# A perceiver block on one core: state-space output projection in plain float32, the gate's low part on GpSimd alone, running products behind the multiplication by the gate

## What is computed

```
proj = h @ in_proj_w.T                        # h: 128 x 512
gate, hBC, dt = split(proj)                   # gate: 128 x 8192
hBC = silu(causal_conv(hBC, 4 taps) + b)      # hs 128 x 8192, B and C 128 x 1024 each
dt = softplus(dt + dt_bias);  X = hs * dt     # 128 heads of 64 columns
M  = (C B^T) * exp(segsum(-exp(A_log) * dt))  # per head, lower triangle: 128 x 128
y  = M @ X + D * hs
xg = y * silu(gate)
xr = xg * rsqrt(mean(xg^2 over a group) + eps)   # 8 groups of 1024 columns
x  = x + (xr * norm_weight) @ out_proj_w.T       # 8192 x 512
```

## Time and profile before

| what | value |
|---|---|
| time, median of 3 runs | 752.7 us |
| the 3 runs | 751.5, 752.7, 756.2 us |
| the profiled execution | 755.4 us |
| its span, first to last instruction | 753.3 us |
| busy share of the span: PE, DVE, ACT, POOL | 95%, 74%, 52%, 40% |
| mean granted clock of PE | 0.982 of full speed |
| read from memory | 93.17 MB, 124 GB/s over the span |

### The profile page before, as it was taken

One profiled execution on the slowest core, in us unless ns is written; L12 is line 12 of the kernel. 1 busy time (PEld: TensorE's weight loads), 2 busy tenths in 40 slices (PEclk: granted clock), 3 DMA queues, 4 the chain that ended last, 5 costly groups with the idle time before them and its releaser, 6 DMA issues.

```text
span 753.3 us, 11908 instructions
## 1 busy us (share of the span) xinstructions
PE 712.1 (95%) x3929; PEld 599.1 (80%) x3929; DVE 553.7 (74%) x1159; ACT 393.6 (52%) x602; POOL 304.9 (40%) x166
## 2 busy tenths in 40 slices
PE   5899999999999999999999999779789999999996
PEld 4678888888888888888888888659778888888885
DVE  6877668658748748747857766468979887888894
ACT  4364445535536546446446444635666666665662
POOL 3352313404404504503413321100577877877772
PEclk9999999999999999999999999898989999999999
DMA  9502021011011001102201104803868777878520
GB/s 330 221 24 70 1 70 65 4 70 56 14 55 70 14 14 63 63 0 70 70 0 70 56 0 194 283 1 118 288 242 333 278 287 277 307 269 298 211 110 14
DMA packets 20290, 93.73 MB, mean 124 GB/s; under 512 B 2608, under 2 KB 3760, under 8 KB 11440
## 3 DMA queue, kind: packets, MB, share of 16 engines
q1 hardware_dynamic: 20272, 93.50, 34.4%
HBM read 93.17 MB, written 0.33 MB: 124 GB/s over the span
## 4 chain that ended last, share of the span: by engine, by line
PE 69%; DVE 16%; issue 6%; ACT 5%; DMA 2%; DVEq 1%; ACTq 0%; SPq 0%; POOL 0%; POOLq 0%
PE bank L379 17%; PE bank L381 17%; PE bank L380 17%; PE bank L489 8%; DVE conv L1282 5%; PE bank L576 3%; DVE decay L1234 2%; ACT y_gT_hi L922 2%; PE bank L459 2%; DMA ctx_raw<-in_ctx_t 1%; DVE y_gT_lo L1269 1%; DVE y L1323 1%; PE bank L658 1%; DVE bank L1317 1%; DMA wqo_raw<-in_wo 1%
## 5 line engine op out<-in xcount | busy, mean ns | idle before, releaser
L1407 POOL TENSOR_TENSOR wqo_lo<-wqo_raw,wqo_hi 128x2048 fp32r<-128x2048 f32 x15 | 69.5, 4633 | 207.4 <-ACT wqo_hi L707 175.7
L1066 DVE TENSOR_TENSOR pt_lo<-bank,pt_hi 128x512 fp32r<-128x512 f32 x128 | 87.8, 690 | 63.2 <-ACT pt_hi L781 63.2
L781 ACT ACTIVATE pt_hi<-bank 128x512 fp32r<-128x512 f32 x128 | 75.8, 598 | 66.8 <-PE bank L489 66.5
L1394 POOL TENSOR_TENSOR k_lo<-rope_a,k_hi 128x512 fp32r<-128x512 f32 x32 | 43.4, 1355 | 107.5 <-ACT k_hi L725 107.5
L1027 DVE CUSTOM_DVE_ANT_0 probs<-bank,mask_sb 128x512 f32<-128x512 f32 x128 | 82.2, 686 | 0.1
L489 PEld LDWEIGHTS bank<-ident,probs 128*128 128x128 f32 x512 | 64.3, 142 | 21.4 <-ACT probs L771 3.9
L489 PE MATMUL bank<-ident,probs 128*128 128x128 f32 x512 | 77.2, 277 | 4.4 <-ACT probs L762 3.5
L1437 POOL TENSOR_TENSOR w_out_lo<-w_out_sb,w_out_hi 128x2048 fp32r<-128x2048 f32 x15 | 70.2, 4681 | 20.2 <-ACT w_out_hi L878 20.1
L771 ACT ACTIVATE probs<-probs,neg_max 128x2048 f32<-128x2048 f32 x31 | 62.0, 2002 | 1.0 <-DVE neg_max L1017 0.6
L576 PE MATMUL bank<-xnT,w_hs_sb 128*128 128x128 f32 x512 | 60.2, 276 | 0.0
L379 PE MATMUL bank<-pt_hi,v_hi 128*128 128x512 f32 x128 | 59.7, 467 | 0.0
(11 more groups left out here) (189 smaller groups left out, 1750.1 us busy)
## 6 DMA issues: line engine op xcount, KB each, us to landing
w_hs_sb<-in_w_hs SPq DMA_DIRECT2D x16, 1024.0 KB, 5.8
w_gate_sb<-in_w_gate SPq DMA_DIRECT2D x16, 1024.0 KB, 5.2
w_out_sb<-in_w_out SPq DMA_DIRECT2D x16, 1024.0 KB, 4.8
wqo_raw<-in_wq SPq DMA_DIRECT2D x8, 1024.0 KB, 4.8
wqo_raw<-in_wo SPq DMA_DIRECT2D x8, 1024.0 KB, 4.8
decay<-decay_rows SPq DMA_DIRECT2D x16, 512.0 KB, 5.5
ctx_raw<-in_ctx_t SPq DMA_DIRECT2D x3, 1024.0 KB, 11.1
wk_raw<-in_wk SPq DMA_DIRECT2D x8, 256.0 KB, 2.7
```

The source lines that it names most:

```text
L781: act.activation(pt_hi[t % 3], ring_b[(t + 1) % 2][:, :], ACT.Copy).then_inc(s["pt_hi_ready"], 1)
L1066: dve.tensor_tensor(pt_lo[t % 3], ring_b[(t + 1) % 2][:, :], pt_hi[t % 3].bitcast(F32), ALU.subtract)\
L1407: pool.tensor_tensor(wqo_lo[:, :, :], wqo_raw[:, :, :], wqo_hi[:, :, :].bitcast(F32), ALU.subtract)\
```

## The change

- out_step multiplies y_gT by w_out_sb in plain float32: 4 matmul calls for a chunk instead of 12. The split parts w_out_hi, w_out_lo and y_gT_lo are gone, with the instructions that made them (L878, L1437, L1269, and L1327 and L1489 for the last chunk). y_gT has two slots.
- The whole of w_gate_lo is made by POOL, 128x2048 in one instruction. DVE's half (L1260) is gone.
- DVE's scan_decay for the next chunk stands behind y = y times gate, not at the head of the next chunk. POOL's product m_t is made in its own chunk, not one chunk ahead.
- Ahead of the chunks: bc_acc and bc_act have memory of their own. ACT makes the first w_gate_hi between the taps of the B and C projections and takes the first taps of hs ahead of two of the four silus. DVE runs the first scan behind the mask product gm. PE runs gate(0) ahead of the transpose of hsT(0), and hs_step of chunk 2 ahead of y(0).
- SP's refill issues the hs weights ahead of the decay rows.

The core of the diff:

```diff
@@ memory
-        w_out_lo = sb("w_out_lo", [P, 2, KC, 512], F32R, mam)
+        w_out_sb = sb("w_out_sb", [P, 2, KC, 512], F32, mam)
...
-        bc_acc = sb("bc_acc", [P, 4 * BCC, P], F32, pre)
-        bc_act = sb("bc_act", [P, 4 * BCC, P], F32, pre)
+        bc_acc = sb("bc_acc", [P, 4 * BCC, P], F32, mam)
+        bc_act = sb("bc_act", [P, 4 * BCC, P], F32, mam)
...
-        y_gT_hi = sb("y_gT_hi", [P, 4, P], F32R, mam)
-        y_gT_lo = sb("y_gT_lo", [P, 4, P], F32R, mam)
+        y_gT = sb("y_gT", [P, 2, 4, P], F32, mam)
@@ SP, refill
+                if hs:
+                    sp.wait_ge(s["hs_mm"], c + 2)
+                    sp.dma_start(w_hs_sb[:, 1 - i, :, :], w_hs[c + 3]).then_inc(hs_in[1 - i], 16)
                 if gate:
                     sp.wait_ge(s["m_ready"], c + 1)
                     load_decay(c + 2, i)
-                if hs:
-                    sp.wait_ge(s["hs_mm"], c + 2)
-                    sp.dma_start(w_hs_sb[:, 1 - i, :, :], w_hs[c + 3]).then_inc(hs_in[1 - i], 16)
@@ PE, out_step
-                    pe.wait_ge(s["wout_lo_ready"], 2 * n + i + 1)
+                pe.wait_ge(wout_in[i], 16 * n + 32)
...
                 for t in range(4):
-                    last = pairs(bank[6][:, :], y_gT_hi[:, t, :], y_gT_lo[:, t, :], w_out_hi[:, i, t, :],
-                                 w_out_lo[:, i, t, :], i == 0 and t == 0, i == 1 and t == 3)
+                    last = pe.matmul(bank[6][:, :], y_gT[:, i, t, :], w_out_sb[:, i, t, :],
+                                     start=i == 0 and t == 0, stop=i == 1 and t == 3)
@@ PE, chunk_step
+                if not first:
+                    transpose_hs(n, i)
                 if first:
                     pe.wait_ge(s["xnT_lo_ready"], 1)
-                    pe.wait_ge(s["first_gate_lo"], 2)
+                    pe.wait_ge(s["first_gate_lo"], 1)
...
                 last.then_inc(s["gate_mm"], 1)
+                if first:
+                    transpose_hs(n, i)
+                    hs_step(1, 0)
                 pe.wait_ge(s["x_ready"], c + 1)
...
-                else:
-                    hs_step(1, 0)
...
-            pe.wait_ge(s["gm_ready"], 2)
@@ ACT
+                if i == 2:
+                    act.wait_ge(gate_in[0], 32)
+                    act.activation(w_gate_hi[:, :, :], w_gate_sb[:, 0, :, :], ACT.Copy)\
+                        .then_inc(s["gate_hi_ready"], 1)
...
-                out_high(n, i)
...
-                at_least(act, s["out_mm"], c)
+                at_least(act, s["out_mm"], c - 1)
                 for t in range(4):
-                    act.activation(y_gT_hi[:, t, :], ygT_bank(t, last_chunk)[:, t * P:(t + 1) * P], ACT.Identity,
+                    act.activation(y_gT[:, i, t, :], ygT_bank(t, last_chunk)[:, t * P:(t + 1) * P], ACT.Identity,
...
+            bc_silu(0)
+            bc_silu(1)
             tap_step(0, 0)
-            act.wait_ge(s["bc_act_ready"], BCC)
-            gate_high(0, 0)
+            bc_silu(2)
+            bc_silu(3)
             silu_step(0, 0)
@@ DVE, chunk_dve
-                if not last_chunk:
-                    scan_decay(n + i, 1 - i)
                 dve.wait_ge(s["hsT_mm"], c + 1)
...
                 dve.tensor_tensor(y[:, i, :], bank[4][:, :], gate[:, i, :], ALU.mult).then_inc(s["y_gated"], 1)
...
-                    gate_low(n + i, 1 - i)
+                if not last_chunk:
+                    scan_decay(n + i, 1 - i)
                 if last_but_one:
                     return
-                ygT_low(n, i, last_chunk)
                 if i == 0 and not first_group:
                     add_group(n - 1)
 
             conv_step(0, 0)
             make_gm()
...
+            dve.wait_ge(s["same_step_ready"], 1)
+            scan_decay(0, 0)
@@ POOL
-                decay_products(n + i, 1 - i)
+                decay_products(n, i)
                 if i == 0 and not (isinstance(n, int) and n == 0):
                     group_norm(n - 1)
-                gate_low_half(n + i, 1 - i)
-                out_low(n, i)
+                gate_low(n + i, 1 - i)
...
             chunk_pool(CH // 2 - 1, 0)
...
+            decay_products(CH // 2 - 1, 1)
             group_norm(CH // 2 - 1)
```

More of the change, by code:

```diff
@@ L609, in out_step @@
                         for t in range(4):
-                            pe.wait_ge(s["ygT_lo_ready"], 4 * (2 * n + i) + t + 1)
-                            last = pairs(dst[:, 0:DM // 2], y_gT_hi[:, t, :], y_gT_lo[:, t, :], w_out_hi[:, i, t, cols],
-                                         w_out_lo[:, i, t, cols], i == 0 and t == 0, i == 1 and t == 3)
+                            pe.wait_ge(s["ygT_ready"], 4 * (2 * n + i) + t + 1)
+                            last = pe.matmul(dst[:, 0:DM // 2], y_gT[:, i, t, :], w_out_sb[:, i, t, cols],
+                                             start=i == 0 and t == 0, stop=i == 1 and t == 3)
                         if i == 1:
@@ L618, in out_step, with transpose_hs @@
                 for t in range(4):
-                    last = pairs(bank[6][:, :], y_gT_hi[:, t, :], y_gT_lo[:, t, :], w_out_hi[:, i, t, :],
-                                 w_out_lo[:, i, t, :], i == 0 and t == 0, i == 1 and t == 3)
+                    last = pe.matmul(bank[6][:, :], y_gT[:, i, t, :], w_out_sb[:, i, t, :],
+                                     start=i == 0 and t == 0, stop=i == 1 and t == 3)
                 last.then_inc(s["out_mm"], 1)
-            def chunk_step(n, i, first, last_chunk):
+            def transpose_hs(n, i):
                 c = 2 * n + i
-                if not last_chunk and not (isinstance(n, int) and n == 0):
-                    hs_step(n + i, 1 - i)
                 pe.wait_ge(s["hs_act"], c + 1)
@@ L631, in chunk_step @@
                 last.then_inc(s["hsT_mm"], 1)
+            def chunk_step(n, i, first, last_chunk):
+                c = 2 * n + i
+                if not last_chunk and not (isinstance(n, int) and n == 0):
+                    hs_step(n + i, 1 - i)
+                if not first:
+                    transpose_hs(n, i)
                 if first:
                     pe.wait_ge(s["xnT_lo_ready"], 1)
-                    pe.wait_ge(s["first_gate_lo"], 2)
+                    pe.wait_ge(s["first_gate_lo"], 1)
                 else:
                     pe.wait_ge(s["gate_lo_ready"], c)
-                    pe.wait_ge(s["gate_lo_half"], c)
                 at_least(pe, s["gate_act"], c)
@@ L869, in gate_high @@
                 act.activation(w_gate_hi[:, :, :], w_gate_sb[:, i, :, :], ACT.Copy).then_inc(s["gate_hi_ready"], 1)
-            def out_high(n, i):
-                act.wait_ge(wout_in[i], 16 * n + 32)
-                if isinstance(n, int) and n == 0:
-                    if i == 0:
-                        act.wait_ge(s["g_mm"], 1)
-                else:
-                    act.wait_ge(s["out_mm"], 2 * n + i - 1)
-                act.activation(w_out_hi[:, i, :, :], w_out_sb[:, i, :, :], ACT.Copy).then_inc(s["wout_hi_ready"], 1)
             def tap_step(n, i):
@@ L1256, in scale_weights @@
                 last.then_inc(s["weights_ready"], 1)
-            def gate_low(n, i):
-                dve.wait_ge(s["gate_hi_ready"], 2 * n + i + 1)
-                dve.tensor_tensor(w_gate_lo[:, i, PAIRS[1], :], w_gate_sb[:, i, PAIRS[1], :],
-                                  w_gate_hi[:, PAIRS[1], :].bitcast(F32), ALU.subtract)\
-                    .then_inc(s["gate_lo_ready"], 1)
-            def ygT_low(n, i, last_chunk=False):
-                c = 2 * n + i
-                for t in range(4):
-                    if last_chunk or t == 0:
-                        dve.wait_ge(s["ygT_hi_ready"], 4 * c + (2 * (t // 2 + 1) if last_chunk else 4))
-                    dve.scalar_tensor_tensor(y_gT_lo[:, t, :], ygT_bank(t, last_chunk)[:, t * P:(t + 1) * P],
-                                             nw[:, bass.ds(4 * c + t, 1)], y_gT_hi[:, t, :].bitcast(F32),
-                                             ALU.mult, ALU.subtract).then_inc(s["ygT_lo_ready"], 1)
             def conv_step(n, i):
@@ L1309, in chunk_dve @@
                 if last_chunk:
-                    ygT_low(n, 0)
                     add_group(n - 1)
@@ L1433, in _ @@
             norm_scale(2)
-            def out_low(n, i):
-                pool.wait_ge(s["wout_hi_ready"], 2 * n + i + 1)
-                pool.tensor_tensor(w_out_lo[:, i, :, :], w_out_sb[:, i, :, :], w_out_hi[:, i, :, :].bitcast(F32),
-                                   ALU.subtract).then_inc(s["wout_lo_ready"], 1)
             def decay_products(n, i):
@@ L1487, in _ @@
             chunk_pool(CH // 2 - 1, 0)
-            pool.wait_ge(s["wout_hi_ready"], CH)
-            pool.tensor_tensor(w_out_lo[:, 1, PAIRS[0], :], w_out_sb[:, 1, PAIRS[0], :],
-                               w_out_hi[:, 1, PAIRS[0], :].bitcast(F32), ALU.subtract).then_inc(s["last_wout_lo"], 1)
+            decay_products(CH // 2 - 1, 1)
             group_norm(CH // 2 - 1)
```

40 lines of the change are left out of this document (10 added, 30 removed).

## The result

The changed kernel takes 745.8 us (median of 5 runs, 740.6 to 746.8) beside 752.5 for the kernel before (751.5 to 756.2); the ratio is 0.988, with a 95% interval of 0.985 to 0.991 (the two medians alone divide to 0.991). A second comparison on another chip gave 0.987 (0.984 to 0.989). The profiled execution took 745.85 us with a span of 744.1, where that of before had 755.4 and 753.3. The forecast was 748.7 us, which is −0.5% of the median of before shown then; the ratio measured is −1.2%.

What follows compares the result with a forecast made beforehand. The DVE loop held PE back in the chunks; freed, PE itself would bind. Terms −1.7, −4.1 and −0.9 sum to −6.7, taken off the profiled 755.4 us: 748.7 us (−0.5%), range 745.0 to 753.3.

Steps and rivals of the forecast that it cites:

- the sum of −6.7 us: Whole kernel: −1.7 for twelve chunks, −4.1 for the first chunks, −0.9 for the last, taken off 755.4.
- The price of a record: PE's float32 out_step: 0.444 us for each 512-column record, 8 records, so 3.55 us a chunk.
- The rival that loads are not hidden: Float32 out_step on PE: weight loads add 0.19 us to each of 128 records, giving 773 us; chance 0.08.
- The loop becomes bound by PE: Steady chunks: PE waits for no other engine, period 12.45 us, every cover above more than a microsecond.
- Term 1: Twelve chunks from 561.81 to 714.07: 150.6 us instead of 152.3, so −1.7.
- 0.25 for each of 5 turns of the loop: Twelve chunks: turns of the loop add 1.2 us to 149.4, making 150.6.
- Term 2: First chunks: transpose of y(1) at 557.7 instead of 561.81, so −4.1, of which 3.0 is clock.
- take 11.0 us, so 540.5: First chunks: hs weights for chunk 2, issued at 529.49, land at 540.5 and delay hs_step for chunk 2.
- faster rival: Hs weights land before 540.5, −2.5 us, and low-clock stretches outside the change are absent, some 2 more: 744 to 746; chance 0.14.
- Term 3: Last chunks, up to DVE's second addition: 27.9 us instead of 28.8, with gate(15) waiting 1.45 for w_gate_lo; −0.9.
- the longest rows: Steady chunks, POOL: with 5.45 and 3.30 us, 0.7 of the 2.5 us margin of m_t is left.
- The chance of a fall of the clock: Rival: PE's new gap from 538.0 to 540.5 halves hs_step of chunk 2's rate, 1.7 to 3.3 us lost; chance 0.20.

Runs made afterwards that it cites:

- scan_mid: Kernel before, split parts kept, DVE's running products moved behind its half of w_gate_lo, ahead of y_gT_lo: 742.9 us, ratio 0.986.
- early_hold: Kernel before, split parts kept, running products right behind y, POOL's w_out_lo held until DVE's half of w_gate_lo is done: 742.1 us, ratio 0.985.
- prologue: Kernel before with float32 out projection, the new order ahead of and in the first chunks and SP's new refill order: 746.9 us, ratio 0.988.
- scan_head: Changed kernel with the scan back at the head of the next chunk and m_t one chunk ahead on POOL: 745.5 us, one run.

## Why the prediction was right in its mechanism and short in its size

The forecast of −0.5% failed at two steps. The first is its level: the sum of −6.7 us was taken off one execution of before that took 755.4, and the result was set beside a median of 752.7, so 2.7 of the 6.7 us were lost. The second is the size of its terms. Against its own profiled execution the sum was −6.7; the profiled execution of after came out at −9.55. The terms below give 4.0 of the difference, a later start takes 1.5 back, and 0.35 lies outside the spans. That the two medians, 752.5 and 745.8, lie 6.7 us apart, as the sum has it, is luck.

- **The price of a record**: 0.444 forecast for 512 columns, 0.436 measured; out_step 3.49 instead of 3.55. The rival that loads are not hidden is out: they take 0.19 each, beside the matmuls.
- **The loop becomes bound by PE**: right, no PE wait at all in eleven chunks. Term 1 was −1.7 and is −3.15. The step that failed is "0.25 for each of 5 turns of the loop", for which the prediction gave no row: chunks alternate between 12.41 and 12.44, so a turn costs 0.03 at most. That is 1.2 of the 1.45; the cheaper record is 0.7, and slightly longer steps elsewhere take 0.45 back.
- **The first chunks**: the order of events was right (weights of chunk 2, then y(0), its transpose, y(1) at full clock). Counted from hs_step(0), Term 2 is −6.2 and not −4.1. The step that failed is the landing "take 11.0 us, so 540.5": they were there 539.97 − 530.99 = 9.0 us behind their issue, 2.0 earlier, and everything behind it is earlier by 2.0 to 2.2. The prediction had named this as the first half of its faster rival (744 to 746 us); the second half, low-clock stretches absent outside the change, did not come, since the trace of after has a clock of 0.51 from 508 to 515.
- **The last chunks**: a wait of 1.0 for w_gate_lo, not 1.45; Term 3 is −1.35, not −0.9.
- **The level**: the gain was 0.9% by its own terms and was written as 0.5%. The 748.7 was kept as a run without the low-clock stretches, though 751.5 had been seen before the change.
- **The reading that fell short** is which edit brings it. The prediction counted float32 as the price of a freed DVE. The runs show that DVE's order alone frees the loop down to 12.0 us a chunk (scan_mid), that one wait more brings 11.73 (early_hold), and that float32 costs PE 0.66 us in each chunk. And the longest rows, 5.45 beside 4.6 for w_out_lo and 3.30 beside 2.4 for m_t, were taken as spread. They were the sign that DVE and POOL stood against each other: in both places POOL's instruction overlaps DVE's w_gate_lo (at 574.26, above, and at 537.70).
- **The chance of a fall of the clock** (0.20) did not come in the changed kernel, whose stop ahead of hs_step(2) was 0.45 us. It did in prologue, where that stop was 2.22 us, and in scan_head at the transpose of y(0), behind a stop of 2.61.

Open: what decides at which stops the clock falls in a run, and what SP's new order brings.
